# Issuing the bursts of typed-row gathers in step with TensorE's batches

## The reference, cut to what matters

```python
src = node_feature[edge_src]
for t in range(n_types):
    msg = jax.nn.relu(src @ W_e[t].T + b_e[t])
    msg = jnp.where((edge_type == t)[:, None], msg, 0)
    parts.append(jax.ops.segment_sum(msg, edge_dst, num_segments=N))
# a later layer
agg = jax.ops.segment_sum(edge_weight[:, None] * support[col], row, num_segments=N)
```

## Time and profile before

| | us |
|---|---|
| three runs | 6973.48, 6984.59, 6986.84 (median 6984.59) |
| span of the profiled execution | 6979.0 |
| adjacency block in it | about 630 to 3379 |
| gathers at L1355 in it | first start 634.6, last start 2036.5 |

### The profile page before, as it was taken

One profiled execution on the slowest core, in us unless ns is written; L12 is line 12 of the kernel. 1 busy time (PEld: TensorE's weight loads), 2 busy tenths in 40 slices (PEclk: granted clock), 3 DMA queues, 4 the chain that ended last, 5 costly groups with the idle time before them and its releaser, 6 DMA issues. The chain is left out here.

```text
span 6979.0 us, 108207 instructions
## 1 busy us (share of the span) xinstructions
PE 4282.9 (61%) x42529; PEld 3047.1 (44%) x42529; DVE 3300.3 (47%) x4529; ACT 1200.2 (17%) x2097; POOL 2026.2 (29%) x2050
## 2 busy tenths in 40 slices
PE   4376111111025555555577777777399988798898
PEld 4254001100025555555466666666255543344344
DVE  8866001100039999999634434333666663012003
ACT  0054000000015555555200000000200011000000
POOL 0324667666640000000355555555100000200200
PEclk9987555555569999999888888888699998899899
DMA  9466333333355555555444444444288855565554
GB/s 316 122 218 202 105 100 123 116 110 118 96 135 215 213 212 217 216 216 211 170 118 119 123 115 125 119 119 123 58 327 302 306 203 184 166 200 176 168 181 154
DMA packets 558978, 1188.75 MB, mean 170 GB/s; under 512 B 168728, under 2 KB 375276, under 8 KB 549516
## 3 DMA queue, kind: packets, MB, share of 16 engines
q1 hardware_dynamic: 427708, 715.31, 31.4%
q10 hardware_dynamic: 60300, 314.88, 11.3%
q0 software_dynamic: 70576, 152.66, 8.7%
HBM read 761.13 MB, written 474.24 MB: 177 GB/s over the span
## 5 line engine op out<-in xcount | busy, mean ns | idle before, releaser
L1401 PE MATMUL psum<-big 128*128 128x98 bf16 x7936 | 897.3, 209 | 968.2 <-DVE big L1383 568.4
L1551 POOL DMA_INDIRECT big<-typed_msgs,big x836 | 827.0, 989 | 2046.8 <-DMA big<-edge_pairs 1676.4
L1401 PEld LDWEIGHTS psum<-big 128*128 128x128 bf16 x7936 | 767.5, 97 | 1040.9 <-DVE big L1383 610.5
L1403 PE MATMUL psum<-big 128*128 128x49 bf16 x7936 | 869.5, 186 | 406.0 <-issue 406.0
L2039 PE MATMUL psum<-big 128*128 128x512 bf16 (+1 forms) x4704 | 1009.0, 375 | 160.6 <-DMA big<-adj 82.2
L1355 POOL DMA_INDIRECT big<-typed_msgs,big x988 | 974.5, 986 | 450.0 <-issue 335.8
L1402 PE MATMUL psum<-big 128*128 128x49 bf16 x7936 | 874.7, 190 | 370.1 <-issue 369.7
L1403 PEld LDWEIGHTS psum<-big 128*128 128x128 bf16 x7936 | 791.6, 100 | 420.6 <-issue 420.6
L1402 PEld LDWEIGHTS psum<-big 128*128 128x128 bf16 x7936 | 771.3, 97 | 414.0 <-issue 414.0
L1378 DVE TENSOR_TENSOR big<-big 128x800 bf16<-128x800 bf16 x496 | 343.3, 692 | 1280.2 <-remote 1077.6
L1644 PE MATMUL psum<-big 128*64 128x128 f32 x3648 | 574.7, 308 | 347.4 <-DVE big L1567 266.8
(11 more groups left out here) (319 smaller groups left out, 3266.8 us busy)
## 6 DMA issues: line engine op xcount, KB each, us to landing
wadj<-big ACTq DMA_DIRECT2D x248, 784.0 KB
big<-wadj SPq DMA_DIRECT2D x124, 1568.0 KB, 7.7
big<-adj SPq DMA_DIRECT2D x210, 896.0 KB
adj<-big ACTq DMA_DIRECT2D x62, 1568.0 KB
big<-staged SPq DMA_DIRECT2D x247, 256.0 KB
staged<-big SPq DMA_DIRECT2D x61, 1024.0 KB
big<-edge_feats SPq DMA_DIRECT2D x456, 128.0 KB
edge_feats<-in_edge_attr SPq DMA_DIRECT2D x1, 51562.5 KB, 163.2
```

Source lines behind the costliest of these rows:

```text
L1401: pe.matmul(to[:, 0:2 * NB], lo, hi_b[:, q, t, 0:2, 0:NB], start=True, stop=False)
L1403: last = pe.matmul(to[:, NB:2 * NB], lo, hi_b[:, q, t, 3, 0:NB], start=False, stop=True)
L1551: pool.indirect_dma_start(out=got4[:, h, u, :], out_offset=None, in_=typed_rows, in_offset=bass.IndirectOffsetOnAxis(ap=pair4i[:, h, u, 0: ...
```

## The change

One line: ahead of burst `h` of pair `i`, GpSimd also waits until TensorE has finished `16*i + 8*h` batches.

```diff
                         pool.wait_ge(s_spair[h], i * (16 * full(h)) + 16 * full(h))
                         at_least(pool, s_sst[h], i * 16)
+                        at_least(pool, s_mm_b, i * (2 * BATCHES) + h * BATCHES)
                         pool.sem_inc(s_turn, 1)
                         for c in range(c0, c1):
                             for u in range(U):
                                 pool.indirect_dma_start(
```

## The result

The changed kernel takes 7047.88 us (7030.73 to 7088.94, four runs) against 6981.62 before: ratio 1.0105, interval 1.0072 to 1.0137. It is one per cent slower; 6410 had been forecast. The profile is of the slowest of the four, 7088.94 us.

What follows compares the result with a forecast made beforehand. Bursts of gathers that follow each other starve TensorE, so gathers and batches run all but serially. 62 cycles of 35 us (burst, drain, uncovered batches) make 2170 us against 2744, 574 less: 6410 us forecast, range 6065 to 6690.

Steps and rivals of the forecast that it cites:

- The burst: First term of a cycle in the adjacency block: sixteen gathers on GpSimd, 22 to 26 us against 20 undisturbed.
- a rule on the shared port: Sign against: GpSimd can't write descriptors while VectorE holds the shared port pair; bursts of 54 us, some 600 us slower.
- GpSimd held off: Rival: VectorE slows every gather in the adjacency block to 2.15 us, cycle 41 us, time 6780; chance 0.09.
- The drain: Second term of a cycle: time from a burst's end until TensorE runs freely, taken as 1.7 us, at most 6.8.
- the uncovered batches: Third term: of a cycle's eight batches, those not done beside the burst, 1.8 to 5.2, at 2.94 us each.
- The fast rival: TensorE hardly notices a lone burst in the adjacency block: cycle 26 to 30 us, 5975 us at 28; chance 0.24.
- The slower rival: A burst starves TensorE at once and drains late: cycle 50.3 us, 7360 us, from under 2.0 batches a burst; chance 0.05.
- Instruction loading: Sign that gathers might delay TensorE's instruction loads: 25 packets load beside gathers, 163 behind them; a lone burst hardly shows.

## Why the prediction was wrong

**What bounds the kernel.** Right for the chip shown: TensorE starved by bursts that follow each other. Incomplete: the second half of the trace, with VectorE busy 1331.8 of 1336 us, holds no gather, so it could not show what a gather meets there. On a quick chip the kernel before is bound by exactly that.

**The burst, first term of the sum: the step that failed.** I took 22 to 26 us from six windows and, as the worst, sixteen gathers of 2.15 us. Each of these rows is from a VectorE that TensorE held up: it was busy for 17.2 of 24.5 us in the first window and for 7.7 to 17.4 in the others. The change was to free TensorE, and that takes VectorE's gaps away. I did set a rule on the shared port against it and named the change's weak side by it, but priced it for each gather apart, at 54 us a burst, and gave "GpSimd held off" 0.09. The price of meeting VectorE isn't the length of an operation: one gather stood for 1409 us, through all batches that were left, because VectorE had no gap before their end.

The rule was also not the one for these operations. The Trainium skill ("SBUF — State Buffer", section on who interferes with whom) says that `tensor_tensor`, which all three operations of a batch are, has no two-port mode, but that with both inputs in SBUF it contends with GpSimd's reads; it infers from this that `tensor_tensor` doesn't hold up the writing of descriptors. Here it is beside just such operations that gathers, which read their row numbers from SBUF, were caught, so the sign came out as the prediction's reading had it. Which port, or whether a port at all, holds them no run shows. The page's measure for the end of a wait, the end of the VectorE operation and some 115 ns (section on the bandwidth-pool intuition), isn't what the traces show when the next operation starts 0.08 us before that end.

**The drain and the uncovered batches.** Right on a starving chip, once no gather is caught. With the pause at each second batch, on a starving chip, the gathers ran from 633.5 to 2646.9 us, 62 cycles of 32.5 us where 35 was forecast. The 61 full bursts last 21.8 to 27.2 us (median 24.0), with 2.8 to 7.8 batches in each (median 5.7), and the store comes 1.6 to 8.4 us behind them (median 1.7). The ratio 0.9107 would make 6361 of 6984.6; the forecast was 6410. Three bounds of the prediction don't follow from its own sum: a cycle of 29.5 gives 6070 (6065 stands there), one of 32 gives 6225 (6200), and one of 39.5 gives 6690 (6680 in one place). None of the three bears on the step that failed.

**The fast rival**, lone bursts nearly free, is what quick chips show (cycle 25.3 with the pause, 1604 us for the block), but on no starving one. **The slower rival** ended on the side where the time did, by another mechanism: the first two bursts of the changed kernel held 250 and 161 matmuls, 5.2 and 3.4 batches, above its limit of 2.0. **Instruction loading**, the other side of the fast rival: the loop on TensorE, starved all the same with 3 packets loaded, rules out slow loading as the cause. What starves TensorE on some chips stays open; it is tied to gathers in flight, builds up over a burst, and four gathers at a time build less of it than sixteen.

**What decides which gather is caught** is narrowed, not settled. GpSimd stands for some 2 us by itself ahead of every 112th gather, numbers 114, 226, 338 and so on, also where VectorE is idle:

```profile
2228.99 0.94 POOL L1355 DMA_INDIRECT big<-typed_msgs,big  x1 [0.30 <-issue]
2232.07 0.94 POOL L1355 DMA_INDIRECT big<-typed_msgs,big  x1 [2.14 <-issue]
```

The caught gather was number 114 or 338 in five of the seven traces, and number 33, the first behind the new wait, in the two of the changed kernel on starving chips. Each of the seven followed a stand of GpSimd of 2.8 to 17 us and started at least 8.5 us into a stretch of VectorE without a gap; no gather for which both held went through. Behind a stand of 1.7 to 2.2 us others went through with VectorE full for 20 to 335 us, and so did the first of the changed kernel's second burst, after 10.6 us, with VectorE full for 3.6. In the traces without a caught gather VectorE had been full for at most 5.6 us when one followed a stand of over 1 us. So the pauses seem to work by keeping such stretches short; that a pause would free a gather once caught, no run shows.

## What to carry to other kernels

When a change frees an engine that was starved, look at which gaps of its neighbours were made by the starvation, and ask who lived on them; rows from the starved stretch can't price what comes after. Where GpSimd issues gathers beside a VectorE that has no pause, give VectorE one a batch (0.13 us here): it cost 0.22 us in a batch of 2.94 and bought 15% of the kernel on one kind of chip. Pacing the gathers is worth 9 to 14% only where gathers starve TensorE, and only with such a pause; in small steps it is worth more than in large ones.

## What the runs showed of the hardware that was not expected

- A gather that GpSimd has begun can stand for 955, 1090, 1288, 1409 or 2661 us, each time until 0.82 or 0.83 us behind the last of VectorE's operations in the block; gathers in a close row go through beside the same VectorE at 1.0 and 1.3 us in turn.
- A pause of 0.13 us a batch is enough to prevent it: with a pause at each batch, or at each second, no trace has a gather of over 2.2 us.
- GpSimd stands for some 2 us ahead of every 112th gather, and where VectorE is full it is behind such a stand, or behind a wait, that a gather is caught.
- The same program takes 6312 to 6319 us on some chips and 6917 to 6984 on others. Most of the difference lies in the two blocks with gathers. The adjacency block took 2563 us against 2749, with TensorE's matmuls coming singly on the second kind. In the block behind, the matmuls took 1121 us (3227.5 to 4348.9) against 1511 (3410.3 to 4920.8), and there TensorE waited 2 us for VectorE on the quick chip and 557 on the first; why isn't known.
